# One transformer layer on one core: the self attention's value blocks are written by DMA into a doubled, zeroed buffer

## The reference, cut to what matters

```python
qkv = ternary_linear(x, w_qkv)
v = qkv[..., Q_SIZE + KV_SIZE:].reshape(bsz, seqlen, NUM_KV_HEADS, HEAD_DIM)
...
attn = jax.nn.softmax(scores, axis=-1)
y = jnp.einsum('bhgqk,bkhd->bqhgd', attn, v).reshape(bsz, seqlen, dim)
return ternary_linear(rms_norm(y), w_proj)
```

## Time and profile before

| | us |
|---|---|
| median of 3 executions | 576.29 |
| all three | 576.29, 575.0, 815.79 |
| the profiled execution, its own time | 573.81 |
| its span, first to last instruction | 572.0 |
| around the span | 1.8 |
| PE busy | 537.9 |
| DVE busy | 445.7 |
| ACT busy | 425.1 |
| POOL busy | 323.4 |

### The profile page before, as it was taken

One profiled execution on the slowest core, in us unless ns is written; L12 is line 12 of the kernel. 1 busy time (PEld: TensorE's weight loads), 2 busy tenths in 40 slices (PEclk: granted clock), 3 DMA queues, 4 the chain that ended last, 5 costly groups with the idle time before them and its releaser, 6 DMA issues. The chain is left out here.

```text
span 572.0 us, 20510 instructions
## 1 busy us (share of the span) xinstructions
PE 537.9 (94%) x7142; PEld 449.1 (79%) x7142; DVE 445.7 (78%) x1389; ACT 425.1 (74%) x1208; POOL 323.4 (57%) x490
## 2 busy tenths in 40 slices
PE   7898999999999999999999999999999999987785
PEld 6687788788887888888888878888888877865564
DVE  2667585888978787888979787878879776889664
ACT  5987898697878878787977787787878777773221
POOL 5241848566565748566555658475665648372610
PEclk9999999999999999999999999999999999999988
DMA  8532503214233231413142332414142404000000
GB/s 253 182 94 100 144 21 101 58 49 102 59 84 81 71 83 37 126 32 90 54 107 59 77 78 46 117 33 107 39 103 58 105 5 113 21 13 21 24 9 10
DMA packets 42805, 42.34 MB, mean 74 GB/s; under 512 B 16080, under 2 KB 33488, under 8 KB 42704
## 3 DMA queue, kind: packets, MB, share of 16 engines
q1 hardware_dynamic: 42704, 41.03, 27.3%
HBM read 38.26 MB, written 2.75 MB: 72 GB/s over the span
## 5 line engine op out<-in xcount | busy, mean ns | idle before, releaser
L874 ACT ACTIVATE pr<-sm,nb 128x257 f32<-128x257 f32 x256 | 129.2, 508 | 9.4 <-DVE nb L1110 8.0
L662 POOL TENSOR_TENSOR cTl<-cx,cTh 128x516 fp32r<-128x516 f32 x64 | 84.3, 1317 | 75.1 <-ACT cTh L771 75.0
L1110 DVE CUSTOM_DVE_ANT_0 sm<-x_ps,mbias 128x257 f32<-128x257 f32 x256 | 99.3, 419 | 21.9 <-PE x_ps L1416 20.2
L771 ACT ACTIVATE pt<-x_ps 128x512 f32<-128x512 f32 x112 | 65.3, 599 | 10.5 <-PE x_ps L1426 6.9
L1426 PE MATMUL x_ps<-tab,pr 128*128 128x128 f32 x512 | 71.4, 274 | 0.8 <-DVE o L1141 0.4
L771 ACT ACTIVATE kk<-x_ps 128x257 f32<-128x257 f32 x128 | 49.5, 389 | 22.1 <-PE x_ps L1308 22.1
L1426 PEld LDWEIGHTS x_ps<-tab,pr 128*128 128x128 f32 x512 | 57.3, 141 | 5.8 <-issue 4.4
L1308 PE MATMUL x_ps<-cTh,wkTh 128*128 128x258 f32 x256 | 59.7, 315 | 0.4 <-ACT pt L771 0.3
L670 POOL TENSOR_TENSOR sr<-sv,halfneg 128x20 f32<-128x20 f32 x16 | 56.7, 3541 | 1.3
L1308 PE MATMUL x_ps<-wvTh,cTh 128*128 128x256 f32 x256 | 56.8, 303 | 0.0
L1308 PE MATMUL x_ps<-cTl,wkTh 128*128 128x258 f32 x256 | 51.4, 282 | 0.6 <-POOL cTl L662 0.6
(11 more groups left out here) (193 smaller groups left out, 1342.7 us busy)
## 6 DMA issues: line engine op xcount, KB each, us to landing
cx<-in_ctx SPq DMA_DIRECT2D x64, 258.0 KB, 3.9
mbias<-mask_bias SPq DMA_DIRECT2D x64, 128.5 KB, 3.4
xq<-in_x SPq DMA_DIRECT2D x16, 128.0 KB, 2.9
xr<-in_x SPq DMA_DIRECT2D x16, 128.0 KB, 2.8
vx<-end_values SPq DMA_DIRECT2D x64, 32.0 KB, 2.3
vr<-self_values SPq DMA_DIRECT2D x64, 32.0 KB, 1.9
out<-yo SPq DMA_DIRECT2D x16, 128.0 KB, 2.6
fraw<-in_L_ffn_w SPq DMA_DIRECT2D x2, 704.0 KB, 5.2
```

Source lines behind the costliest of these rows:

```text
L662: g.tensor_tensor(cxbuf(cT[1], b)[:, :, :], cx[:, b % BT, :, :], cxbuf(cT[0], b)[:, :, :].bitcast(F32), ALU.subtract).then_inc(A_ctl, 1)
L771: return sc.activation(dst, src, ACT.Copy)
L874: sc.activation(pr[:, b % 2, gr, :], sm[:, b % 2, gr, :], ACT.Exp, bias=nb[:, n:n + 1], scale=-1.0, accum_out=st[:, 0, b, gr:gr + 1]).then ...
L1110: v.tensor_tensor_reduce(out=sm[:, b % 2, gr, :], in0=xb(f"S{b}", gr)[:, 0:LK], in1=mbias[:, b, :], scale=1.0, scalar=0.1 * NEG, op0=ALU.a ...
```

## The change

Five edits:

1. `vr` is dropped, and `vbd` becomes 128 x (2 buffers, 4 blocks h, 4 batches, 64 columns), 8 KB in each partition where `vr` and the old `vbd` took 5 KB.
2. POOL zeroes the whole of `vbd` once, with a memset ahead of the first step's list (semaphore `W_vz`).
3. The four DMAs of `B_shuffle` write straight into `vbd`: DMA h into block h of the buffer i % 2, on partitions h*32 to h*32+31. The other blocks of these partitions stay zero. They wait for the product of two tiles ago (`B_pv`, i - 2), or for `W_vz` in the first two tiles.
4. `D_vbd` is dropped from POOL's lists, all 16 of them.
5. `D_PV` waits for `L_vr` in the place of `B_vbd`, and reads its 64 moving columns as 4 runs of 16 floats, 1 KB apart.

```diff
-            ("PX", 0), ("CL", 2), ("CL", 3), ("D_vbd",), ("Q_root",), ("B_root",), ("PX", 1), ("CL", 4),
+            ("PX", 0), ("CL", 2), ("CL", 3), ("Q_root",), ("B_root",), ("PX", 1), ("CL", 4),
...
-        vr = sb("vr", [P, BT, KV * HD])
-        vbd = sb("vbd", [P, BT * KV, 4, HD])
+        vbd = sb("vbd", [P, 2, 4, BT, KV * HD])
...
                         sp.dma_start(v_dram, qs[:, NQK * HD:QKV]).then_inc(L_vw, 16)
                         sp.wait_ge(L_vw, 16 * i)
-                        if due(i - 1):
-                            sp.wait_ge(B_vbd, i - 1)
+
+                        if due(i - 2):
+                            sp.wait_ge(B_pv, i - 2)
+                        else:
+                            sp.wait_ge(W_vz, 1)
                         for h in range(4):
-                            sp.dma_start(vr[h * S:(h + 1) * S, :, :],
+                            sp.dma_start(vbd[h * S:(h + 1) * S, i % 2, h, :, :],
                                          v_dram.rearrange("(b k) d -> k b d", b=BT)).then_inc(L_vr, 16)
...
             for b in range(1, BT):
                 q_blocks(0, b)
+            g.memset(vbd[:, :, :, :, :], 0.0).then_inc(W_vz, 1)
             pool.wait_ge(L_gain, 16)
...
-                    elif k == "D_vbd":
-
-                        pool.wait_ge(L_vr, 64 * i1)
-                        if due(i1 - 1):
-                            pool.wait_ge(B_pv, i1 - 1)
-                        g.tensor_tensor(
-                            vbd[:, :, :, :],
-                            vr[:, :, :].rearrange("p b (j d) -> p (b j) d", d=HD).unsqueeze(2).to_broadcast([P, BT * KV, 4, HD]),
-                            m4.unsqueeze(1).unsqueeze(3).to_broadcast([P, BT * KV, 4, HD]), ALU.mult
-                        ).then_inc(B_vbd, 1)
...
                         pe.wait_ge(B_p4, i1)
-                        pe.wait_ge(B_vbd, i1)
+                        pe.wait_ge(L_vr, 64 * i1)
                         (was_read, n_read), = read("D_PV")
                         pe.wait_ge(was_read, n_read)
                         for j in range(KV):
                             for b in range(BT):
                                 last = mm(xb("D_PV")[b * S:(b + 1) * S, j * 64:(j + 1) * 64], p4[:, b * KV + j, :],
-                                          vbd[:, b * KV + j, :, :].rearrange("p h d -> p (h d)"), start=True, stop=True)
+                                          vbd[:, i1 % 2, :, b, j * HD:(j + 1) * HD], start=True, stop=True)
                         last.then_inc(B_pv, 1)
```

More of the change, by code:

```diff
@@ L265 @@
             (1, "EX"), (2, "CL", 2), (2, "CL", 3), (2, "PX", 0), (2, "Q_root"), (1, "QBD", 2), (2, "B_root"),
-            (2, "PX", 1), (2, "D_vbd"), (1, "QBD", 3), (2, "CL", 4), (2, "B_rope"), (2, "CL", 5), (2, "D_yroot"),
+            (2, "PX", 1), (1, "QBD", 3), (2, "CL", 4), (2, "B_rope"), (2, "CL", 5), (2, "D_yroot"),
             (2, "B_qkroot"), (2, "PX", 2), (2, "D_xroot"), (2, "PX", 3), (2, "QBD", 0), (2, "QBD", 1), (2, "EX"),
@@ L275 @@
         "last": [
-            (14, "Q_root"), (14, "CL", 2), (14, "PX", 0), (14, "CL", 3), (14, "D_vbd"), (14, "PX", 1),
+            (14, "Q_root"), (14, "CL", 2), (14, "PX", 0), (14, "CL", 3), (14, "PX", 1),
             (14, "B_root"), (14, "B_qkroot"), (14, "CL", 4), (14, "D_yroot"), (14, "QBD", 0), (14, "B_rope"),
             (14, "PX", 2), (14, "PX", 3), (14, "CL", 5), (14, "EX"), (14, "D_xroot"), (14, "QBD", 1), (15, "CL", 2),
-            (15, "CL", 3), (15, "PX", 0), (14, "QBD", 2), (15, "B_root"), (14, "QBD", 3), (15, "D_vbd"),
+            (15, "CL", 3), (15, "PX", 0), (14, "QBD", 2), (15, "B_root"), (14, "QBD", 3),
             (15, "PX", 1), (15, "B_qkroot"), (15, "D_yroot"), (15, "PX", 2), (15, "B_rope"), (15, "PX", 3),
-            (15, "EX"), (15, "D_xroot"), (16, "D_vbd"), (16, "B_root"), (16, "B_rope"), (16, "D_yroot"),
-            (16, "B_qkroot"), (16, "D_xroot"), (17, "D_vbd"), (17, "D_yroot"), (17, "D_xroot"),
+            (15, "EX"), (15, "D_xroot"), (16, "B_root"), (16, "B_rope"), (16, "D_yroot"),
+            (16, "B_qkroot"), (16, "D_xroot"), (17, "D_yroot"), (17, "D_xroot"),
         ],
@@ L470, in perceiver @@
         T_cast, T_dve = sig("T_cast"), sig("T_dve")
-        W_mb, W_vxp, W_vx = sig("W_mb"), sig("W_vxp"), sig("W_vx")
+        W_mb, W_vxp, W_vx, W_vz = sig("W_mb"), sig("W_vxp"), sig("W_vx"), sig("W_vz")
         F_dve = [sig(f"F_dve{n}") for n in range(3)]
@@ L498, in perceiver @@
         B_ra, B_rb, B_rc, B_rr = sig("B_ra"), sig("B_rb"), sig("B_rc"), sig("B_rr")
-        B_qTp, B_qTs, B_kTp, B_kbd, B_vbd = sig("B_qTp"), sig("B_qTs"), sig("B_kTp"), sig("B_kbd"), sig("B_vbd")
+        B_qTp, B_qTs, B_kTp, B_kbd = sig("B_qTp"), sig("B_qTs"), sig("B_kTp"), sig("B_kbd")
         B_sp, B_s2, B_mx, B_s3, B_p2 = sig("B_sp"), sig("B_s2"), sig("B_mx"), sig("B_s3"), sig("B_p2")
```

## The result

The changed kernel takes 572.23 us (median of 9 runs, 570.77 to 573.1), the kernel before 574.77 us in the same session (9 runs, the one of 815.79 us among them; without it the median is 574.75). The ratio is 0.9959, with a 95% interval of 0.9946 to 0.9971: a gain of 0.4%, small but real. The forecast was 573.7 us. It started from a median of 575.6 for the kernel before, which was 0.8 us too high. As a ratio it said 0.9967, and that lies inside the interval. The profiled execution took 572.17 us with a span of 570.4; that of before took 573.81 with 572.0. The sum had said 571.9.

What follows compares the result with a forecast made beforehand. PE was taken to bound the repeated steps, leaving gains only at the ends. 573.81 - 1.5 - 0.4 = 571.9 us for the profiled execution; with ordinary runs 1.8 higher, the median forecast was 573.7 us, range 568.5 to 579.

Steps and rivals of the forecast that it cites:

- its two causes: Masked copy on POOL: it stalls DVE's `xn` in step 2 and `x1` in step 16; removal gains 1.9 us.
- Step 2: DVE's `xn`, stalled by POOL's copy, ends earlier without it, so PE's transpose gains 1.5 us, bounds 0 and 1.65.
- Step 16: DVE's `x1`, stalled by POOL's copy, is shorter without it; what follows comes 0.4 us earlier, bounds 0 and 0.47.
- Repeated steps: Eleven steps from 100 to 460 us: PE itself is the bound, so removing POOL's copy gains 0.
- The rival by which more is freed: Repeated steps: POOL's 31.5 us let DVE and PE close gaps, at most 5.0 us, to 568.7; chance 0.08.
- Memset: Kernel start on POOL: zeroing `vbd` takes 2.5 us, hidden ahead of PE's first waiting product; cost 0, at worst some tenths.
- DMAs and their wait: Writes into `vbd`: neither the wait for the product of two tiles ago nor the product's wait for DMAs costs anything, 0.
- strided read: `D_PV` on PE: reading 64 moving columns as 4 runs of 16 costs 0, up to 3.7 us over 512 records.
- The rival with 3.7 us: `D_PV` on PE: runs cost what the row allows, 3.7 us on the forecast, 577.4 us; chance 0.10.
- the one with each run as a product of its own: `D_PV` on PE: four runs cost 42.4 ns a record instead of 13.9, 14.6 us more, 588.3 us; chance 0.04.
- The tail: Kernel end: shifts by 1.9 us with the same PE clock dip; another dip costs about 1.3 us, none gives as much back.

Runs made afterwards that it cites:

- qbd_first: The kernel before, with only the masked copy of step 2 moved behind POOL's `qbd` instruction: 573.0 us, 0.9976 of the kernel before.
- memset_2_16: The changed kernel plus a POOL memset of 2048 elements to a scratch tile in steps 2 and 16: 573.82 us, 0.9997 of the kernel before.
- copy_rest: The changed kernel plus a scratch copy like the masked one in the 14 steps other than 2 and 16: 572.86 us, 0.9969 of the kernel before.
- after_again: The changed kernel unaltered, run once more in another session: 572.2 us, 0.9950 of the kernel before.
- after_third: The changed kernel unaltered, run a third time beside a kernel with filler products: 571.18 us, 0.9941 of the kernel before.

## Why the prediction came out

It was right in its two causes, and its size came out within the range. The gain forecast was 1.9 us and the measured ratio gives 2.4; of the 1.5 us between 573.7 and 572.23, 0.8 is the starting median. A range of ten microseconds around an effect of two would have held nearly any outcome, so what bears the prediction out are its terms. One reading of its rows was off: PE's slices stand at 9 from the fifth to the thirty-fifth, not from the fourth to the thirty-eighth; no term hangs on it.

*Step 2, 1.5 us, bounds 0 and 1.65.* The term was right: 1.58, 1.55 and 1.56 us in three profiles of the changed kernel, and 1.58 from the order alone (qbd_first). It let `qbd` block `xn`, which it does (0.62 us), and took the difference of the ends of `xn` as PE's gain. By its own rows that looks too small: `xn` was to end at 85.2, PE was ready at 85.5, and nothing would have been left to wait for. What it did not see is DVE's score entry behind `xn`, whose bank the transpose needs and which puts the transpose 0.45 us behind the end of `xn`, before and after. 85.2 + 0.45 is 85.65, that is 1.5 us ahead of 87.16. So the difference of the ends was the right measure, for a reason that the prediction did not give; that part was luck.

The Trainium skill, page "SBUF — State Buffer", section "Who interferes with whom", was cited with the prediction. Its rule that one side keeps the ports for the whole instruction agrees with every row here: `x1` ends 0.27 to 0.29 us after the copy in the four profiles that show it, whatever it overlaps, and a memset blocks `xn` as a copy does (1.99 us against 2.18). That the first to be issued keeps them is not what the start times show: `xn` starts 0.06 us ahead of the copy in the profile of before and 0.04 us ahead of the memset in memset_2_16, and it is the one that stands still. Either a start in the profile is not yet a hold on the ports, or the start order isn't what decides; no run here tells which.

*Step 16, 0.4 us, bounds 0 and 0.47.* 0.48, 0.47 and 0.47 us by the table, the upper end.

*Repeated steps, 0.* Right: 354.79 of 360 us busy for PE against 355.01, the wait for `xn` unchanged, and in copy_rest the copies cost nothing that stands out from the third tile to the fourteenth, with a median 0.7 us above that of the changed kernel and intervals that overlap. The rival by which more is freed falls: all of POOL's copies in these steps lay in its idle time.

*Memset, 0, price taken 2.5 us.* It took 1.80 us. Timeline of the changed kernel (POOL, then PE):

```profile
13.55 1.80 POOL L696 MEMSET vbd<- 128x2048 f32 x1
...
15.68 1.28 POOL L664 TENSOR_TENSOR cTl<-cx,cTh 128x516 fp32r<-128x516 f32 x1
...
19.96 0.80 PE L1301 MATMUL x_ps<-cTh,wkTh 128*128 128x258 f32 x2
```

The context's low part came 0.65 us later than in the earlier trace rows and ended at 16.96, 3.0 us before PE's first product. A memset eight times as large takes 5.8 times as long, so scaling by elements was the nearest of the three prices and still too dear.

*DMAs and their wait, 0; strided read, 0, up to 3.7.* Both 0: PE has no wait for a DMA of `vbd` in the list of waits, and the product's durations are 218/219/245 ns after and 219/219/243 before. The rival with 3.7 us and the one with each run as a product of its own, which would have ended slower, fall with this.

*The tail.* In this pair of profiles the dip moved along, as expected: 0.56 from 550 to 553 us before, and 1.65 us earlier in the changed kernel nearly the same, with PE again busy 2.8 of 3 us:

```profile
548.35:551.35 3.00, 2.81 (x15) 1.88 (x13) 1.45 (x4) 1.92 (x5) 0.74 (x2) 0.55 0.00 0
```

That was luck. In the two other profiles of the changed kernel the clock falls elsewhere in the tail: after_again shows 0.86 from 520 to 530 us and 0.69 from 565 to 570, after_third 0.50 from 540 to 545 and 1.00 from 550 to 553. Their tails are 0.8 and 0.3 us longer against the last `xn`; the prediction had this as a reason to widen the range.

*What is left.* The sum gave 1.9 us and the profiles 1.6, with a dip at the start of the changed kernel's and none at the start of the other; by the three ratios of the changed kernel (0.9959, 0.9950, 0.9941) the gain is 2.4 to 3.4 us, with 2.0 found in the two stalls. The difference is of the size of the dips at the start and in the tail and of the scatter, and no run here resolves it.

## What to carry to other kernels

Don't count what a relieved engine saves; find its instructions that overlap a stretched one on the bounding path. Here two of sixteen copies carried the gain, and they were visible before the change as two outliers in the durations of DVE's instructions (2179 and 894 ns against medians of 328 and 424). Before removing work for such a stall, try the order: one swapped pair of neighbours in POOL's list gave about half of the gain by the ratios. A small wait that is left in a tuned steady state may be the short side of a balance, and moving one entry to close 0.7 us opened 2.0.

## What the runs showed of the hardware

Beside one long instruction of POOL the two DVE instructions looked at here stood to its end: `xn` (2.18 us beside a copy of 1.97, 1.99 beside a memset of 1.80, which only writes; median 0.33) and `x1` (0.72 to 1.02 us beside the copy; median 0.42; never seen beside a memset). In the one case on record where two of POOL's followed each other without a gap, the waiting `xn` went through between them (0.61 us, qbd_first). A memset of 2048 elements in each partition took 1.80 us, in floats and in bf16 alike. A product's moving operand in four runs of 64 bytes, 1 KB apart, ran as fast as in one run (0.219 us for a record both times). And the granted clock fell to 0.66 to 0.70 between 20 and 25 us in one profile of a kernel and not in the next, with all that follows 0.6 to 1.3 us later: profiles that differ by less should be compared step by step, not by their spans.
